# A two-layer graph network: sums of layer 2's weight blocks made in stage 2 and kept in DRAM

## The reference

```python
def _sage_sum(h, src, dst, Ws, Wn, b):
    h_neigh = jax.ops.segment_sum(h[src], dst, num_segments=N_NODES)
    return h @ Ws + h_neigh @ Wn + b
h = _sage_sum(h, src, dst, Ws1, Wn1, b1)
h = _sage_sum(h, src, dst, Ws2, Wn2, b2)
return x + h
```

## Time and profile before

| | us |
|---|---|
| median of 3 runs | 696.12 |
| lowest and highest | 695.1, 699.23 |
| the profiled execution | 695.65 |
| its span (first to last instruction) | 693.8 |
| PE busy / POOL busy / ACT busy / DVE busy | 651.5 / 173.2 / 174.7 / 320.8 |

### The profile page before, as it was taken

The page is one execution under the profiler, slowest core; times in us unless marked ns, Lnnn a source line. Parts: engine busy times, 40 slices in busy tenths (PEclk is TensorE's granted clock), DMA queues, the critical chain, the costliest instruction groups (busy, mean ns, idle before and its releaser), DMA issues.

```text
span 693.8 us, 8548 instructions
## 1 busy us (share of the span) xinstructions
PE 651.5 (94%) x3280; PEld 562.4 (81%) x3280; DVE 320.8 (46%) x426; ACT 174.7 (25%) x292; POOL 173.2 (25%) x161
## 2 busy tenths in 40 slices
PE   3899999999999999999999489998999986999997
PEld 2788778887999999999999377886877765888886
DVE  2733798770010100101112985878578799611111
ACT  4444233222110210211024133332433425100000
POOL 5524244000000000000005297965414157000000
PEclk9999999999999999999999799999999998999999
DMA  8522231002211112112129733443122520011111
GB/s 286 182 52 52 72 101 46 31 32 71 72 38 52 47 37 67 30 37 67 30 63 349 254 115 133 160 139 122 46 77 76 168 92 31 8 69 53 50 61 59
DMA packets 58110, 61.15 MB, mean 88 GB/s; under 512 B 16033, under 2 KB 34475, under 8 KB 58070
## 3 DMA queue, kind: packets, MB, share of 16 engines
q1 hardware_dynamic: 58070, 60.63, 26.9%
HBM read 50.10 MB, written 10.51 MB: 87 GB/s over the span
## 4 chain that ended last, share of the span: by engine, by line
PE 73%; issue 9%; POOL 8%; DVE 3%; DMA 3%; SPq 2%; ACT 1%; DVEq 0%; POOLq 0%
PE PS L1120 16%; PE PS L1032 14%; PE PS L1170 13%; PE PS L1128 13%; PE PS L1154 12%; PE PS L1024 3%; POOL right_sum L645 3%; POOL left_sum L634 3%; POOL s L623 2%; DMA xin<-x_in 1%; PE PS L1058 1%; SPq L432 1%; SPq L398 1%; DMA right_sum<-wn_in 1%; DVE left L994 1%
## 5 line engine op out<-in xcount | busy, mean ns | idle before, releaser
L1154 PE MATMUL PS<-right,left 128*128 128x512 f32 x840 | 202.7, 403 | 23.1 <-DVE right L997 9.4
L1154 PEld LDWEIGHTS PS<-right,left 128*128 128x128 f32 x840 | 163.0, 196 | 62.5 <-issue 18.6
L1032 PE MATMUL PS<-W,HT 128*128 128x512 f32 (+1 forms) x480 | 123.0, 405 | 3.4 <-issue 2.4
L1120 PE MATMUL PS<-HT,W_st 128*128 128x416 f32 (+1 forms) x576 | 110.6, 352 | 0.9 <-issue 0.9
L1120 PEld LDWEIGHTS PS<-HT,W_st 128*128 128x128 f32 x576 | 108.2, 188 | 2.3 <-issue 1.4
L1032 PEld LDWEIGHTS PS<-W,HT 128*128 128x128 f32 (+1 forms) x480 | 87.8, 190 | 23.1 <-issue 2.8
L1128 PE MATMUL PS<-AT,y_st 128*128 128x416 f32 (+2 forms) x480 | 92.3, 352 | 0.0
L1128 PEld LDWEIGHTS PS<-AT,y_st 128*128 128x128 f32 (+1 forms) x480 | 90.3, 188 | 0.8
L997 DVE TENSOR_TENSOR right<-right_sum,right 128x512 fp32r<-128x512 f32 x56 | 60.8, 1091 | 39.1 <-ACT right L798 38.6
L1170 PE MATMUL PS<-y_high,AT 128*128 128x512 f32 (+1 forms) x200 | 78.3, 392 | 0.0
L1170 PE MATMUL PS<-y_low,AT 128*128 128x512 f32 (+1 forms) x200 | 78.3, 392 | 0.0
(11 more groups left out here) (78 smaller groups left out, 471.1 us busy)
## 6 DMA issues: line engine op xcount, KB each, us to landing
raw<-wn_in SPq DMA_DIRECT2D x40, 256.0 KB, 2.9
raw<-ws_in SPq DMA_DIRECT2D x32, 256.0 KB, 2.9
y_dram<-y_out SPq DMA_DIRECT2D x18, 256.0 KB, 2.0
y_st_raw<-y_dram SPq DMA_DIRECT2D x8, 576.0 KB
s<-x_in SPq DMA_DIRECT2D x18, 256.0 KB
out<-s SPq DMA_DIRECT2D x18, 256.0 KB
W_raw<-wn_in SPq DMA_DIRECT2D x16, 256.0 KB, 3.9
xin<-x_in SPq DMA_DIRECT2D x8, 512.0 KB, 11.9
```

Of the source, the lines that this page charges most:

```text
L1032: ins = nc.tensor.matmul(PS[:r, bank, :], HT[:, a, k, t * P:t * P + r], W[:, k, b, :], start=first and m == 0, stop=last and m == 2)
L1120: ins = nc.tensor.matmul(PS[:, banks[c], 0:w_], W_st[:, a, k, :], HT[:, b, k, o_:o_ + w_], start=k == 0 and m == 0, stop=False)
L1154: ins = nc.tensor.matmul(PS[:, BANKS2[g % 8], :], left[:, k, a, i * P:(i + 1) * P], right[:, KB - 1 - k, b, :], start=k == 0 and j == 0, s ...
```

## The change

The 40 right operands that are sums are made during stage 2, and both of their parts are kept in DRAM (`sums_dram`, 512 KB each). `prep` is a ring of five slots for them in SBUF. SP runs `prepare(i)`: it waits until slot i % 5 is stored (`prep_stored`, from i = 5 on), loads the two blocks of sum i, then waits for the low part of sum i - 4 (`prep_lo`) and stores that sum's two parts. POOL adds (all 40 sums, ahead of its first work on h1), ACT makes the high part, DVE the low part. `PER_TILE = (3, 4)` sets the places: in SP's program, three `prepare` behind the `y_st` load of tile j, and four behind the `W_st` load of tile j + 1; on ACT and DVE, three behind the split of `W_st` for tile j + 1, four behind the split of `y_st` for tile j + 1 (on ACT also behind `h1_save(j)`). With seven for a tile, the sums 0 to 39 belong to tiles 0 to 5. Four more calls of `prepare` in tile 6 only store.

In layer 2, SP loads a sum's two parts in one DMA of 512 KB straight into `right`, and PE waits for that load (`right_in`). POOL, ACT and DVE have no work on it. Right operands that are no sums go on as before. DVE's bias for half 1 moves from n = KB - 1 to n = KB. The loops of ACT and DVE over the feature tiles are written out.

```diff
-RAW_SLOTS = 3
-EARLY_RAW = KB
+PREP = 5
+PER_TILE = (3, 4)
+def prepared(j, part):
+    first = j * sum(PER_TILE) + part * PER_TILE[0]
+    return range(first, min(first + PER_TILE[part], len(sum_steps())))
...
 (SP)
+            def prepare(i):
+                if i < len(sum_steps()):
+                    if i >= PREP:
+                        sp.wait_ge(prep_stored[i % PREP], 16 * (i // PREP))
+                    for which in range(2):
+                        quarter(sum_steps()[i], which, prep_raw[:, i % PREP, 1 - which, :]).then_inc(prep_in[i % PREP], 16)
+                if i >= PREP - 1:
+                    e = i - (PREP - 1)
+                    sp.wait_ge(prep_lo, e + 1)
+                    sp.dma_start(sums_dram[e, :, :, :], prep[:, e % PREP, :, :].bitcast(F32)).then_inc(prep_stored[e % PREP], 16)
             for j in range(KF):
                 if j:
                     sp.wait_ge(wst_used, j)
                     load_w_st(j)
+                    for i in prepared(j - 1, 1):
+                        prepare(i)
                 ...
+                for i in prepared(j, 0):
+                    prepare(i)
+                if j == KF - 2:
+                    for i in range(PREP - 1):
+                        prepare(len(sum_steps()) + i)
             def load_right(n):
+                if n >= KB:
+                    wait_step(sp, n - KB)
+                elif n == KB - 1:
+                    sp.wait_ge(h1_done, KF)
                 if right_is_sum(n // KB):
-                    ...
+                    sp.dma_start(right[:, KB - 1 - n % KB, :, :].bitcast(F32), sums_dram[right_sums(n), :, :, :]).then_inc(right_in[n % KB], 16)
 (POOL)
+            for i, n in enumerate(sum_steps()):
+                pool.wait_ge(prep_in[i % PREP], 32 * (i // PREP + 1))
+                nc.gpsimd.tensor_tensor(prep_raw[:, i % PREP, LO, :], prep_raw[:, i % PREP, LO, :], prep_raw[:, i % PREP, HI, :],
+                                        RIGHT[SEQUENCE[n // KB][1]][2]).then_inc(prep_summed, 1)
 (ACT)
+            for j in range(KF - 1):
+                w_st_high(j + 1)
+                for i in prepared(j, 0):
+                    prepare_high(i)
+                y_st_high(j + 1)
+                h1_save(j, j % 2)
+                for i in prepared(j, 1):
+                    prepare_high(i)
 (DVE, layer 2)
-                if n == KB - 1:
+                if n == KB:
                     for t in range(NT):
                         add_bias(t)
-                dve.wait_ge(right_hi, n + 1)
-                nc.vector.tensor_tensor(right[:, KB - 1 - k, LO, :], ...
+                if not right_is_sum(p):
+                    ...
 (PE)
-                    pe.wait_ge(right_lo, p * KB + k + 1)
+                    if right_is_sum(p):
+                        pe.wait_ge(right_in[k], 16 * (p + 1))
```

More of the change, by code:

```diff
@@ L94, in right_sums, with sum_steps @@
     return sum(right_is_sum(q // KB) for q in range(n))
-def right_copies(n):
-    return sum(not right_is_sum(q // KB) for q in range(n % KB, n + 1, KB))
+def sum_steps():
+    return [n for n in range(STEPS) if right_is_sum(n // KB)]
+def prepared(j, part):
+    first = j * sum(PER_TILE) + part * PER_TILE[0]
+    return range(first, min(first + PER_TILE[part], len(sum_steps())))
 def evictions():
@@ L226, in gnn_kernel @@
     y1_dram = nc.dram_tensor("y1_dram", (N, D), F32, kind="Internal").ap()
+    sums_dram = nc.dram_tensor("sums_dram", (len(sum_steps()), P, 2, HALF), F32, kind="Internal").ap()
     ctx = ExitStack()
@@ L472, in _, with quarter @@
                     sp.dma_start(AT[:, :, t * P:(t + 1) * P].bitcast(F32), any_cols[:, :, :]).then_inc(g_written, 16)
+            def quarter(n, which, to):
+                what, m = SEQUENCE[n // KB]
+                row, col = RIGHT[m][which]
+                return sp.dma_start(to, (ws2 if what == "s" else wn2)[row * HALF + n % KB * P:row * HALF + (n % KB + 1) * P,
+                                                                      col * HALF:(col + 1) * HALF])
+            def prepare(i):
[8 more added lines that the diff above has]
+                    sp.dma_start(sums_dram[e, :, :, :], prep[:, e % PREP, :, :].bitcast(F32)).then_inc(prep_stored[e % PREP], 16)
             for j in range(KF):
@@ L755, in _, with prepare_high @@
             y_st_high(0)
-            with act.Fori(0, KF // 2 - 1) as q:
-                for parity in range(2):
-                    stationary_high(2 * q + parity + 1)
-                    h1_save(2 * q + parity, parity)
-            stationary_high(KF - 1)
-            h1_save(KF - 2, 0)
+            def prepare_high(i):
+                act.wait_ge(prep_summed, i + 1)
+                nc.scalar.activation(prep[:, i % PREP, HI, :], prep_raw[:, i % PREP, LO, :], ACT.Copy).then_inc(prep_hi, 1)
+            for j in range(KF - 1):
[6 more added lines that the diff above has]
+                    prepare_high(i)
             def evict(p):
@@ L779, in _ @@
             act.wait_ge(h1_padded, 1)
+            for i in range(PREP):
+                act.wait_ge(prep_stored[i], 16 * (len(sum_steps()) // PREP))
             for n in range(STEPS):
@@ L944, in _, with prepare_low @@
                                                     any_key[:, bass.ds(pair * 2 + odd, 1), i], None, ALU.is_equal).then_inc(g_ready, 1)
-            with dve.Fori(0, KF) as j:
+            def prepare_low(i):
+                dve.wait_ge(prep_hi, i + 1)
+                nc.vector.tensor_tensor(prep[:, i % PREP, LO, :], prep_raw[:, i % PREP, LO, :], prep[:, i % PREP, HI, :].bitcast(F32),
+                                        ALU.subtract).then_inc(prep_lo, 1)
+            for j in range(KF):
                 dve.wait_ge(wst_hi, j + 1)
@@ L949, in _ @@
                                         ALU.subtract).then_inc(wst_lo, 1)
+                if j:
+                    for i in prepared(j - 1, 0):
+                        prepare_low(i)
                 dve.wait_ge(yst_hi, 2 * j + 2)
```

80 lines of the change are left out of this document (23 added, 57 removed).

## The result

The changed kernel takes **743.51 us** (median of 4 runs, 742.36 to 745.81) against 697.67 of the kernel before (4 runs, 695.1 to 701.18) on the same chip: ratio 1.0658, 95% interval 1.0599 to 1.0716. It is slower by 46 us; the forecast was 713, in a range of 697 to 734. The direction was right, the size was not.

The account below looks back on a forecast made before the run. The prediction took stage 2 as bound by PE and layer 2 as losing 34.5 us to PE's gaps and half clock. From the profiled 695.65, minus 31 in layer 2 plus 49 in stage 2 gave 713.7, said as 713; range 697 to 734.

Parts of the forecast that it names:

- That stage 2 pays for the sums, through SP's order: Stage 2: SP waits out a whole store in every prepare call, ahead of loads PE needs; 49 us lost.
- The price of a call, 4.1 us: SP in stage 2: 0.80 us issuing two loads, store landed at 4.0, 0.1 for the wait; floor 3.5, ceiling 5.1.
- A: SP's round in stage 2: the issue of the W_st load; from it to the last store's issue 17.7 us.
- B: SP's round in stage 2: the issue of the y_st load; from it to the round's end 18.0 us.
- ceiling for stage 2: Stage 2: upper bound on the loss, +79 us, at 5.1 us a call, for stores between loads.
- rival 3: Stage 2: stores behind loads take longer, or DRAM mixes reads and writes slower; 5.1 us a call, total 743, chance 0.12.
- Rivals 1 and 2: Stage 2: stores land sooner, total 693, chance 0.18; or SP's round fits into the tile, total 672, chance 0.07.
- rival 4: Layer 2 keeps its transitions, POOL's left sums and y2's splits in the way: gain 15 to 20, total 725 to 729, chance 0.10.
- The floor: Stage 2: lower bound on the loss, 3.5 us a call, round 31.5, tile 6's W_st issue at 344, +28 us.
- Layer 2, 31 us gained, 194 to 196 in all: Layer 2: PE's idle gaps and half clock mostly go, 3.5 us left over; bounds of the gain 20 and 33.5.
- The first gap: Layer 2: DVE's ten biases wait for x ahead of a split; the gap goes, 9.35 us and 2.5 of clock.
- The signs named: PE idles in stage 2 for W_st (some 5 us) and y_st (some 4), not in tile 7; W_st issues 34 to 37 apart.

Follow-up runs that it names:

- e4: The changed kernel with eight slots for sums in place of five, the store still four sums behind: 695.82 us.
- e8: The changed kernel with each prepare call loading one block of 256 KB in place of two, output wrong: 717.18 us, median of three executions of four.
- e5: The changed kernel with eight slots in place of five and the store six sums behind in place of four: 666.15 us.
- e1: The kernel before, with only DVE's ten biases on x's half 1 moved from n = KB - 1 to n = KB: 698.65 us.
- e7: The changed kernel with DVE's bias on half 1 moved back to n = KB - 1: 746.12 us.
- e9: The kernel before, with the bias at n = KB and x's right half fetched early, some raw loads left out, output wrong: 695.42 us.
- e10: The changed kernel with eight slots in place of five and each sum stored five calls behind its loads: 671.86 us.

## Why the prediction was right in its sign and wrong in its size

**That stage 2 pays for the sums, through SP's order: right.** The forecast named the wait (a slot's reuse waits for the store just issued) and the stalled loads behind it. The waits of SP's queue show it 34 times, and giving it more slots removes 48 us (e4).

**The price of a call, 4.1 us: the step that failed.** It had a store behind its call's two loads land 3.2 us after its issue; the trace has 4.1 to 4.4 in the round shown, so a call behind a call takes 4.9 to 5.2. In the round shown above, counted from A = 226.27 and B = 247.05:

| | forecast | measured |
|---|---|---|
| the store issued before A lands | A + 2.9 | A + 4.2 |
| the next ones | 8.3, 12.4, 16.5 | 9.2, 14.4, 19.4 |
| B | A + 17.7 | A + 20.8 |
| first store behind B is issued | B + 10.0 | B + 10.9 |
| its landing, the next | 12.7, 16.8 | 13.5, 18.7 |
| next A | B + 18.0 | B + 20.0 |

A store with nothing just ahead of it landed in 2.61 us, where 2.7 was forecast from the earlier trace rows, and the wait for the first low part was read within 1 us. What was too short is the landing behind the call's own two loads, worked out with the engines at 387 GB/s as in the earlier trace rows. In a window of after with one such call, 1.05 MB, the traffic lies spread over some 4 us of 0.15 us slices:

```profile
GB/s 0 0 0 0 0 0 0 82 205 273 355 396 314 232 232 287 273 246 219 341 328 355 451 437 396 451 328 273 164 109 109 82 55 0 0 0 0 0 0 0
```

That is 1.05 MB in 3.9 us, about 269 GB/s, where 387 were taken: the traffic ends 4.9 us after the call's first issue (198.79 to 203.65) and not 3.6 after it. The store at 257.93, which has the engines to itself, passes its 0.52 MB in 1.35 us, 388 GB/s. So the term that was too small is the traffic time of two loads and a store together, 2.7 us for a measured 3.9. Rounds were 41.8 us in the mean against 35.7: four full rounds make 24.4 us, the first, shorter one 5.0, and the later issue of tile 1's `W_st` (188.23 for 186.3) 1.9: these are the 31 us by which the stage ended later than forecast (453.4 against 421.9). Half of the load's bytes take a third of this excess away (e8), at the same low rate; what lowers the rate when loads and a store follow each other stays open.

The Trainium skill, DMA: Bandwidth & Descriptors, section Anatomy of one DMA, would give an estimate of 3.2 us for 512 KB by its fit (2.0 us and 436 KB a microsecond), for a path that this kernel does not use. The trace's lone store took 2.61, shorter. Those behind loads took 4.1 to 4.4, longer, and an estimate for one DMA alone says nothing of that.

**The bounds and the rivals.** The forecast's own ceiling for stage 2 was +79, at 5.1 a call, and 78.4 is what it lost: rival 3 (743 us, chance 0.12) is what happened. Its two forms, stores behind loads take longer and a lower rate for reads beside writes, are not told apart: a call's bytes pass at 262 to 269 GB/s, but that is no ceiling, for in e5 317 GB/s of loads and stores pass beside each other over 40 us. The range cut that rival off with the argument that no row showed it. That was so, but neither did a row show the opposite: the 2.0 us of the earlier trace rows is what a store takes by itself, and even the one of 3.9 us (issued at 167.97, no traffic from 167 to 168) has nothing just ahead of it. The one hint in the trace of before lies outside the group: the store issued at 90.90, with a load issued 0.37 us behind it, landed after 2.5 us and not 2.0. The price was extrapolated at the full rate, and the slow side of it should have stayed in the range. Rivals 1 and 2, sooner landings or a round that fits, fell, and so did rival 4: of layer 2's transitions, waits of 0.3 and 1.6 us are left. The floor has a slip: A of tile 6 at 344 gives, with the forecast's own 7.9 and two tiles, +31 and not +28. The miss does not hang on it.

**Layer 2, 31 us gained, 194 to 196 in all: right, with one wrong reason.** Measured 30.4 and 195.15; the splits of right parts left DVE and the late evictions went. 2.6 us of PE's idle time are left, where 3.5 were allowed with a slow window. The first gap, 9.35 us, was put down to the bias ahead of a split. e1 and e7 say that its place is worth nothing, and e9 that it hangs on x's landing together with POOL's sums. The forecast did have x land early too, up to 2 us ahead of layer 2 for a measured 0.7 behind its start, but it sized the term by the gap itself. So this term came out right for whichever reason the gap went, in part by luck.

**The signs named.** PE idles before L1146 and L1154 (of before: L1120, L1128) and not in the last tile: right. Some 5 us for `W_st`: 3.65 to 4.46. Some 4 for `y_st`: 3.6 in the first, then 7.2 to 9.5, since B came 3 us late and `y_st` was ready 10.3 after B. `W_st` issues 34 to 37 apart: 38.0 to 43.2. The half clock behind each wait is hidden by SP's pace, as forecast: SP waited for PE once, just ahead of the first round.

## What to carry to other kernels

In a ring of slots that one queue both fills and drains, count two distances: from a store's issue to the reuse of its slot, and from a load to the store that waits for its result. Both must exceed, in calls, the latency between them at the stage's pace; here three more slots and a store six calls behind turned +46 us into -32 without a byte less. And price a DMA at the latency that it has behind its own neighbours; where no row shows that, keep the slow side in the range.

## What the runs showed of the hardware that was not expected

- A store of 512 KB landed 2.61 us after its issue with no load just ahead of it, 4.0 in the median behind one load of 256 KB, 4.4 behind two (e8, after). Where SP waits least and the engines are 96% busy (e5) the median is 6.2. The call's bytes pass at 269 GB/s behind two loads and 262 behind one; a store by itself passes at 388.
- Issuing took longer while other transfers were under way: a pair of loads takes 0.80 us of SP's time in after, where SP has just waited for a landing, and up to 2.44 in e10, behind a `W_st`.
- Ten f32 additions of 128x512 on DVE took 6.11 us in e7 and 15.89 in e9, where POOL adds all the time and its sum of the same size went from 1.28 to 1.74. In e7 it was POOL that waited: its sum of 128x640, begun at 458.55 beside the last additions, took 5.17 us, where 1.6 is the median and the same sum in after took 2.12. The Trainium skill, SBUF — State Buffer, section SBUF: two separate sides, says that a DVE operation with two SBUF inputs and a GpSimd operation that reads SBUF contend for one pair of ports, and whichever starts first has it for its whole instruction. The traces agree in kind: in e9 DVE pays 1.0 us more for each addition and POOL 0.46 more for a sum, in e7 POOL pays 3.6 and DVE nothing.
